# First-layer experts: the second bias loaded over all partitions and added by VectorE, in place of a three-row product on TensorE

## The reference

```python
logits = jnp.einsum('btd,de->bte', x, gate_W) + gate_b
top1 = jnp.argmax(logits, axis=-1).reshape(-1)
flat_x = x.reshape(b * t, d)
for e in range(num_experts):
    mask = (top1 == e).astype(x.dtype)[:, None]
    h = jax.nn.gelu(flat_x * mask @ W1[e] + b1[e], approximate=False)
    out = out + (h @ W2[e] + b2[e]) * mask
```

## Time and profile before

| | us |
|---|---|
| median of three timed runs | 2732.41 |
| profiled execution | 2740.07 |
| its span (first to last instruction) | 2738.0 |
| TensorE busy | 2513.4 (92%) |
| VectorE busy | 1468.3 (54%) |
| ScalarE busy | 1090.1 (40%) |
| the 23 tiles of this stage, first load wait ended to last output taken | 1394.24 to 1578.58 |

### The profile page before, as it was taken

How to read it: one execution, slowest core, us unless ns; L and a number is a source line. 1 busy time by engine, 2 the same in 40 slices (tenths; PEclk the granted TensorE clock), 3 DMA queues, 4 the chain that set the end, 5 groups by cost and what they waited for, 6 DMA issues and landing times. The chain is left out here.

```text
span 2738.0 us, 40280 instructions
## 1 busy us (share of the span) xinstructions
PE 2513.4 (92%) x16447; PEld 1513.1 (55%) x16447; DVE 1468.3 (54%) x2148; ACT 1090.1 (40%) x1881; POOL 702.0 (26%) x383
## 2 busy tenths in 40 slices
PE   7879999999999999999979968999899998799998
PEld 4356534754375535753368834463453634588887
DVE  5768447952877367843821134556455555644442
ACT  3675345732664256533412213544345443011111
POOL 0147036910965056802700020000000000022222
PEclk9989999999999999999989977999999998899999
DMA  4555202100030003100069920010100102055553
GB/s 158 217 198 201 90 1 110 51 9 0 1 144 24 1 0 120 40 9 0 8 240 329 336 49 9 1 34 15 24 24 1 25 8 100 16 163 169 175 174 82
DMA packets 74590, 229.61 MB, mean 84 GB/s; under 512 B 12341, under 2 KB 41354, under 8 KB 57642
## 3 DMA queue, kind: packets, MB, share of 16 engines
q1 hardware_dynamic: 62362, 203.91, 20.9%
q0 software_dynamic: 8784, 15.61, 2.5%
q10 hardware_dynamic: 3264, 7.56, 0.7%
HBM read 170.40 MB, written 52.44 MB: 81 GB/s over the span
## 5 line engine op out<-in xcount | busy, mean ns | idle before, releaser
L687 PE MATMUL psum<-arena 128*128 128x512 f32 (+4 forms) x3776 | 1040.5, 428 | 55.8 <-ACT arena L1597 8.8
L687 PEld LDWEIGHTS psum<-arena 128*128 128x128 f32 x3776 | 618.6, 194 | 414.2 <-issue 306.3
L2616 POOL TENSOR_TENSOR arena<-arena 128x1024 f32<-128x1024 f32 x128 | 299.4, 2371 | 118.1 <-DVE arena L2098 80.5
L2098 DVE TENSOR_TENSOR_SCAN arena<-arena,psum 128x512 f32<-128x512 f32 x256 | 291.0, 1201 | 21.9 <-PE psum L851 14.9
L851 PEld LDWEIGHTS psum<-arena 128*128 128x128 f32 x2048 | 237.1, 193 | 49.1 <-ACT arena L1622 40.3
L851 PE MATMUL psum<-arena 128*128 128x128 f32 x2048 | 249.3, 279 | 2.0 <-issue 1.9
L2657 POOL DMA_INDIRECT arena<-xn,arena x32 | 31.7, 990 | 791.1 <-DVE arena L2554 783.8
L2210 DVE SCALAR_TENSOR_TENSOR arena<-psum,arena 128x1024 f32<-128x1024 f32 x128 | 155.9, 1244 | 93.8 <-PE psum L1014 93.4
L2627 POOL TENSOR_TENSOR arena<-arena 128x1024 f32<-128x1024 f32 x32 | 75.7, 2367 | 429.6 <-ACT arena L1721 429.6
L1896 ACT ACTIVATE arena<-psum 128x256 f32<-128x256 f32 x128 | 49.1, 383 | 297.0 <-PE psum L687 291.3
L1721 ACT ACTIVATE arena<-arena 128x1024 f32<-128x1024 f32 x128 | 147.1, 1149 | 44.4 <-DVE arena L2210 43.1
(11 more groups left out here) (305 smaller groups left out, 3077.1 us busy)
## 6 DMA issues: line engine op xcount, KB each, us to landing
arena<-in_W SPq DMA_DIRECT2D x46, 1024.0 KB
slots_x<-arena SPq DMA_DIRECT2D x9, 1920.0 KB, 16.1
arena<-c_rows SPq DMA_DIRECT2D x32, 512.0 KB, 4.0
arena<-in_Wg SPq DMA_DIRECT2D x16, 1024.0 KB, 4.9
arena<-in_Wu SPq DMA_DIRECT2D x16, 1024.0 KB, 7.5
arena<-in_Wd SPq DMA_DIRECT2D x16, 1024.0 KB, 9.9
arena<-in_xT SPq DMA_DIRECT2D x8, 512.0 KB, 5.1
zs_all<-arena SPq DMA_DIRECT2D x4, 1024.0 KB, 3.9
```

The lines of the kernel that those rows point to most:

```text
L687: r = mm(dst, w, x, start=i == 0, stop=i == len(pairs) - 1)
L2098: V.tensor_tensor_scan(hs[n % 3][:, c, :], dA[n % 2][:, c, :], bank[4 + c], 0.0, ALU.mult, ALU.add)\
L2616: nc.gpsimd.tensor_tensor(h, h, c_all[:, n % CBUFS, :].unsqueeze(1).broadcast_to([P, 2, L]), ALU.mult)\
```

## The change

The three-row product and all that prepares it go. `b2b` becomes a tile of 128 partitions by 256 in f32. SP loads into it the expert's row of `b2` from the input, read 128 times (128 rows of 1 KB in place of three rows of 512 B). The first instruction of L1113 opens the accumulation. VectorE, which had copied the output out of psum, adds `b2b` as it takes it. The load stays the last of its group, and all the buffers behind `b2b` move by 256 words in each partition.

```diff
-        b2_parts = nc.dram_tensor("b2_parts", (E0, 3, D), bf16, kind="Internal").ap()
...
-        b2f, b2s = w_g[0:E0, 0, 0:D], w_g[0:E0, 1, 0:3 * P].bitcast(bf16).rearrange("p (k n) -> p k n", k=3)
...
-        b1b, b2b = [take(KH) for _ in range(2)], [take16(D) for _ in range(2)]
+        b1b, b2b = [take(KH) for _ in range(2)], [take(D) for _ in range(2)]
...
-            for dst, src in ((const, "consts"), (vec, "vecs"), (b2f, "b2")):
+            for dst, src in ((const, "consts"), (vec, "vecs")):
...
-                if b3 == 0:
-                    sp.wait_ge(m_step.sem, 5)
-                    sp.dma_start(b2_parts, b2s).then_inc(a_st_rest.sem, 16)
-                    sp.wait_ge(a_st_rest.sem, 16)
...
-                                 (b2b[j][0:3, :], b2_parts[bass.ds(e, 1)].rearrange("a k n -> (a k) n"))):
+                                 (b2b[j], A["b2"][bass.ds(e, 1)].broadcast_to([P, D]))):
...
-                mm(y, ones16[0:3, :], b2b[j][0:3, :], start=True, stop=False)
...
-                    r = mm(y, h0T[j][:, m, :], w2b[j][:, m, :], start=False, stop=m == KH - 1)
+                    r = mm(y, h0T[j][:, m, :], w2b[j][:, m, :], start=m == 0, stop=m == KH - 1)
...
-            def split_b2():
-
-                for k in range(3):
-                    link(m_step, V.tensor_copy(b2s[:, k, :], b2f))
-                    if k < 2:
-                        link(m_step, V.tensor_tensor(b2f, b2f, b2s[:, k, :], ALU.subtract))
...
-                    split_b2()
...
-                V.tensor_copy(y0[j], bank[4 * j + 3][:, 0:D]).then_inc(wb_free.sem, 1)
+                V.tensor_tensor(y0[j], b2b[j], bank[4 * j + 3][:, 0:D], ALU.add).then_inc(wb_free.sem, 1)
```

More of the change, by code:

```diff
@@ L791, in _ @@
                         if s == 0:
-                            pe.wait_ge(ld_const.sem, 48)
+                            pe.wait_ge(ld_const.sem, 32)
                         for c in range(NC):
@@ L1564, in _ @@
                 if s == 0:
-                    act.wait_ge(ld_const.sem, 48)
+                    act.wait_ge(ld_const.sem, 32)
                 if 0 <= b2 < B:
@@ L1637, in _ @@
                 w(LV.drained, LV.upto("out", 2))
-                act.wait_ge(a_st_rest.sem, 32)
+                act.wait_ge(a_st_rest.sem, 16)
                 norm_roots(0, hb)
@@ L1972, in _ @@
                 if s == 0:
-                    dve.wait_ge(ld_const.sem, 48)
+                    dve.wait_ge(ld_const.sem, 32)
                     V.tensor_copy(ident16, ident)
```

## The result

The changed kernel has a median of 2746.1 us (six runs, 2737.6 to 2751.5), the kernel before 2733.7 in the same series: ratio 1.0044, interval 1.0030 to 1.0057. It is slower, by 9 to 12 us. The profiled execution took 2747.18 us (span 2745.1).

What follows compares the result with a forecast made beforehand. TensorE was taken to bound nearly everything, with DMA near full in the experts' stage and about every other tile waiting for loads. Terms 1.4 - 1.6 + 0.4 + 0.2 = +0.4 us on 2732.41 gave 2732.8, range 2729 to 2738.5.

Steps and rivals of the forecast that it cites:

- (c): DMA queues: the wider load, last of its group, adds 0.40 us per pair with a wait, bounds 0 to 0.65.
- (a): TensorE: dropping the 23 three-row products saves 0.20 us per tile, bounds 0 to 0.37.
- (b): VectorE: an add replaces the copy out of psum, same shape, at cost 0.
- (d): Early in the program: five small VectorE operations and SP's store go, hidden, so 0; else a gain of 1.66 us.
- (e): First tile: TensorE waits for the same group of loads, so +0.40 - 0.20 = +0.2 us.
- Rival 1: In 16 tiles beside ScalarE's weight loads, DMA engines become the bound: +5.4 us, +9.6 at 0.65 a tile; chance 0.22.
- Rival 2: Experts' stage: the 128 KB load hides in DMA gaps and TensorE's saving stays, -3.2 us, 2729.2; chance 0.14.
- rival 3: TensorE: the saving does not come, as the weight load shows instead, +3.6 us, 2736.0; chance 0.08.

Runs made afterwards that it cites:

- e3: The changed kernel with the semaphore split: TensorE waits for W1 and b1 before the hidden values, W2 and b2 only before the second products; ratio to before 0.9943.
- e4: The changed kernel with b2 on its own semaphore, which VectorE waits for before its add in place of TensorE; ratio to before 0.9992.
- e2: The kernel before plus a load per tile of the b2 row, read 128 times into a spare buffer that TensorE waits for; ratio 1.0037.
- e14: The changed kernel with the wide load doubled to 128 packets of 2 KB, 256 KB, from another tensor; ratio to before 1.0035.
- e6: The changed kernel with b2b loaded from 128 distinct rows of DRAM in place of one row read 128 times; ratio to before 1.0037.
- e12: The changed kernel with the wide load cut to 128 of 256 columns, 128 packets of 512 B, 64 KB; ratio to before 1.0019.
- e8: The changed kernel with the wide load cut to 16 rows, 16 KB, still last in its group; ratio to before 0.9987.
- e9: The changed kernel with the split wait of e3 and each tile's token load issued one tile earlier; ratio to before 0.9947.
- e1: The changed kernel without the load per tile: both b2b buffers loaded once, VectorE's add kept; ratio to before 0.9987.
- e5: The kernel before, bias product kept, with the split wait of e3; ratio to before 0.9955.
- e13: The changed kernel with the wide load cut to 64 of 128 rows, 64 packets of 1 KB, 64 KB; ratio to before 0.9999.

## Why the prediction was wrong

The forecast was +0.4 us with a range to 2738.5; it came to 2746.1.

- **What bounds the stage: right.** Loads for the tile after next, a chain from the take of an output to the landing of its group, waits in about every other tile: the trace after shows the same in the main, with 12 waits in 22 intervals, and e3 and e4 show that the waiting and not the traffic makes the loss. That a tile which waited spares the next one its wait is not strict: in the kernel before two tiles in a row waited already (7.89 and 8.93 in the earlier trace rows), and after four times.
- **(c), the step that failed: the load's price.** 0.40 us for each waited pair was 131 KB at the stage's rate, and with the tiles that were to wait anew and the first one the sum had 3.6 us for the load (7 x 0.40 + 0.4 + 0.4). With nothing else changed (e2) the load cost 10 us: 10.3 us more waiting on 12 waits in place of 8, and two falls of the clock. Divided by the 12 waited tiles, 10.3 us is 0.9 us; divided by all 22 intervals it is 0.47, near my 0.40. So e2 alone would also allow a right price that was counted for too few tiles. But such a price, of bytes, would have doubled in e14, and it didn't; as far as the intervals of e6 and e12 to e14 tell, the price goes neither by bytes nor by the packets' time, and the bounds of 0 to 0.65 were those of a quantity that doesn't set it. That the source row's 128-fold reading costs nothing held (e6).
- **What the sum had no term for: the clock.** Two waits in e2, and three in each of the changed kernel's two profiled executions, had the hidden values at 5.3 to 5.5 us in place of 3.84 behind them. These waits were of 1.9 to 3.6 us. That is 1.5 to 1.6 us each, 4.7 us of the changed kernel's stage. No wait before was over 1.4 us, so the trace of before could not show it, but its first tile could have warned: its weight loads took 5.87 us in place of 3.75, behind a wait of 3.98 us, and the mean clock there was 0.82.
- **(a), PE's saving: too small in size, too large in worth.** I took 0.20, the spacing seen, under a bound of 0.37; it was 0.40. The rest is 0.10 of the 0.32 us between the transposes and the bias product, and 0.10 in the 16 products behind it, for which I had no term. The last tile has no transposes ahead of it and gained as much: 7.04 in place of 7.45 where it doesn't wait (e3, e8, e9). But I let 16 stretches keep the saving in full. e1 shows what it is worth without the load: 3.6 us timed, of 9 that 23 x 0.40 would be. A faster tile is less time for the next loads; waits there went from 6.8 to 12.9 us. That the sum had 3.2 us for it (16 x 0.20), so near the 3.6, is luck: half the size, kept too often.
- **(b) held, (d) as far as can be seen.** The add takes 421 ns, the copy took 425. The start and round s = 2 gave nothing that can be told from the noise of executions.
- **(e)** came out at +1.0 us in place of +0.2: PE's wait for the first group took 4.4 us in place of 3.6, which is more than the 0.40 of its bytes.
- **Rival 1** had the sign, and by chance of its arithmetic a time near (2737.8, or 2742 at the higher price), but not the mechanism. It said that the DMA engines would be full and waits come in nearly every tile. They come in 12 of 22, and the share from 1420 to 1540 went down (0.90, 0.90, 0.95). Full engines are what e3 has. **Rival 2** is out by e2, **rival 3** by the 7.26.
- The Trainium skill's 358 GB/s for HBM (DMA: Bandwidth & Descriptors, "Where 436 GB/s comes from") is not met as a limit here: e3 holds 370 to 372 GB/s over 120 us. These rates are not of reads alone, as the stage's stores to `slots_y` are in them.

**What stays open.** Why 128 packets more delay the chain by some 0.9 us a waited tile. Two observations, not tried further: SP's issue of a load, 0.33 to 0.38 us, now and then took 0.5 to 2.0 (1.34 in the fence above, ahead of a 2.1 us wait), which would fit a queue that is full. But it doesn't go with the loss: e2 had one such issue of 0.48 alone and lost as much, e5 had one of 1.53 and no wait, and in e13 nearly every tile had one of 0.5. And no row tells the 16 engines apart, so whether one or two of them land late can't be said from here.

## What to carry to other kernels

Before a load is widened, ask what waits for it, not what it weighs: when a semaphore gathers several loads and its waiter stands on the critical path, the last landing is the price, and here it was twice the bytes' time for each tile that waited. Put each load's wait where its data is first read; splitting one wait took 12 us off the kernel before, and brought the changed kernel from 9 to 12 us above it to 16 us below it, more than any choice of how to add the bias. And a saving on the engine that waits for a chain shortens the time that the chain has; count it only where no wait follows.

## What the runs showed that I had not expected

- Waits of TensorE within a busy stretch can cost more than their length: of the 35 waits of 1.87 to 3.83 us ahead of the hidden values, behind the first output, over the changed kernel and the experiments, 21 had slower hidden values behind them (1.4 to 1.6 us lost, 2.95 once; in the fence above the granted clock was 0.58 of full speed) and 14 had not. None of the shorter ones had. Length alone doesn't decide it: 1.87 and 1.92 us had it, 2.74 and 3.09 had not.
- A three-row bf16 product between f32 ones cost 0.40 us a tile, though its own row says 0.28 and the next product started 0.20 after it: 0.10 us ahead of it and 0.10 in the 16 products behind it left with it.
- One row of DRAM read 128 times had longer packets than 128 distinct rows (all 1 KB packets of the queue 56.2 and 47.1 ns on average), and the two kernels took the same time (1.0033 and 1.0037).
- The same 64 KB was 0.2% of the whole program dearer as 128 packets of 512 B than as 64 of 1 KB (intervals 1.0009 to 1.0028 and 0.9989 to 1.0009).
